# A graph layer's layer norm: centring moved from VectorE to ScalarE, epsilon from GpSimd to VectorE, a negation on GpSimd, and the start-up rearranged

## The reference, cut to what matters

```python
def _layernorm(x, axis=-1, eps=1e-05):
    m = jnp.mean(x, axis=axis, keepdims=True)
    v = jnp.var(x, axis=axis, keepdims=True)
    return (x - m) / jnp.sqrt(v + eps)

def reference(x, adj, W, b):          # x 4096 x 256, adj 4096 x 4096, W 256 x 256
    h = jnp.maximum(_layernorm(x), 0.0)
    out = jax.nn.relu(jnp.matmul(jnp.matmul(adj, h), W.T) + b)
    return x + out
```

## Time and profile before

| what | before |
|---|---|
| median of 3 runs | 383.32 us (382.74 to 383.51) |
| the profiled execution, device time | 382.79 us |
| its span in the trace | 381.0 us |
| PE (TensorE matmuls) busy | 376.3 us, 99% |
| DVE (VectorE) busy | 218.1 us, 57% |
| ACT (ScalarE) busy | 170.9 us, 45% |
| POOL (GpSimd) busy | 63.0 us, 17% |
| granted TensorE clock | 1.00 throughout |

### The profile page before, as it was taken

One profiled execution on the slowest core, in us unless ns is written; L12 is line 12 of the kernel. 1 busy time (PEld: TensorE's weight loads), 2 busy tenths in 40 slices (PEclk: granted clock), 3 DMA queues, 4 the chain that ended last, 5 costly groups with the idle time before them and its releaser, 6 DMA issues.

```text
span 381.0 us, 4425 instructions
## 1 busy us (share of the span) xinstructions
PE 376.3 (99%) x1649; PEld 308.2 (81%) x1649; DVE 218.1 (57%) x293; ACT 170.9 (45%) x197; POOL 63.0 (17%) x79
## 2 busy tenths in 40 slices
PE   8999999999999999999999999999999999999996
PEld 4888888888888888888888888888888888888885
DVE  5999999994745353535564535353565344444424
ACT  4656655654553434343644343434364334343414
POOL 2787777760010000000001000000000100000000
PEclk9999999999999999999999999999999999999999
DMA  7987778669649565656565856565657675656203
GB/s 235 372 288 263 261 267 268 209 201 321 204 156 348 175 214 175 209 179 209 175 207 184 312 178 210 177 211 173 212 174 209 239 255 181 210 181 205 68 2 110
DMA packets 23062, 80.25 MB, mean 211 GB/s; under 512 B 2496, under 2 KB 3264, under 8 KB 23040
## 3 DMA queue, kind: packets, MB, share of 16 engines
q1 hardware_dynamic: 21024, 72.36, 58.0%
q0 software_dynamic: 2016, 7.60, 5.5%
HBM read 75.76 MB, written 4.19 MB: 210 GB/s over the span
## 4 chain that ended last, share of the span: by engine, by line
PE 99%; DVE 0%; ACT 0%; issue 0%
PE bank L379 92%; PE bank L420 6%; PE bank L429 1%; ACT out_sb L355 0%; DVE out_sb L292 0%; DVE warm L256 0%
## 5 line engine op out<-in xcount | busy, mean ns | idle before, releaser
L379 PE MATMUL bank<-adj_hi,h_sb 128*128 128x512 f32 x1024 | 255.1, 390 | 0.0
L223 DVE TENSOR_TENSOR adj_lo<-adj_in,adj_hi 128x1024 fp32r<-128x1024 f32 x126 | 154.2, 1224 | 138.6 <-ACT adj_hi L313 138.5
L379 PEld LDWEIGHTS bank<-adj_hi,h_sb 128*128 128x128 f32 x1024 | 192.3, 188 | 40.7 <-ACT h_sb L323 0.9
L313 ACT ACTIVATE adj_hi<-adj_in 128x1024 fp32r<-128x1024 f32 x126 | 133.4, 1059 | 160.7 <-PE bank L379 157.4
L379 PE MATMUL bank<-adj_lo,h_sb 128*128 128x512 f32 x512 | 137.9, 389 | 0.0
L379 PEld LDWEIGHTS bank<-adj_lo,h_sb 128*128 128x128 f32 x512 | 96.0, 188 | 20.5 <-DVE adj_lo L228 0.6
L203 POOL TENSOR_TENSOR rstd<-var_eps,minus_half 128x1 f32<-128x1 f32 x32 | 49.5, 1546 | 2.5
L215 POOL DMA_DIRECT2D out_t_dram<-out_sb x3 | 2.2, 723 | 209.7 <-DVE out_sb L292 209.7
L323 ACT ACTIVATE h_sb<-centred,rstd 128x256 fp32r<-128x256 f32 x32 | 16.3, 509 | 24.2 <-POOL rstd L203 24.0
L292 DVE TENSOR_TENSOR out_sb<-out_sb,xt_sb 128x512 f32<-128x512 f32 (+1 forms) x17 | 11.1, 659 | 7.7 <-ACT out_sb L355 7.7
L355 ACT ACTIVATE out_sb<-bank,b_sb 128x512 f32<-128x512 f32 (+1 forms) x17 | 11.3, 664 | 9.2 <-PE bank L420 9.2
(11 more groups left out here) (20 smaller groups left out, 31.6 us busy)
## 6 DMA issues: line engine op xcount, KB each, us to landing
adj_in<-adj_t_dram SPq DMA_DIRECT2D x126, 512.0 KB, 3.8
xt_sb<-x_t_dram POOLq DMA_DIRECT2D x4, 1024.0 KB, 7.2
x_sb<-x_dram SPq DMA_DIRECT2D x7, 512.0 KB, 6.5
out_t_dram<-out_sb POOLq DMA_DIRECT2D x3, 1024.0 KB, 5.0
adj_in<-adj_t_dram SPq DMA_DIRECT2D x4, 256.0 KB, 4.3
out_t_dram<-out_sb SPq DMA_DIRECT2D x3, 256.0 KB, 2.0
x_sb<-x_dram SPq DMA_DIRECT2D x4, 128.0 KB, 4.4
w_sb<-w_t_dram POOLq DMA_DIRECT2D x1, 256.0 KB, 5.2
```

The costliest lines, as they stand in the source:

```text
L223: nc.vector.tensor_tensor(adj_lo[:, k, :], adj_in[:, k, :], adj_hi[:, k, :].bitcast(fp32), ALU.subtract).then_inc(s_lo, 1)
L313: nc.scalar.activation(adj_hi[:, k, :], adj_in[:, k, :], ACT.Copy).then_inc(s_hi, 1)
L379: last = nc.tensor.matmul(bank(g, kb, c)[:], h_sb[:, t, hp, kb * P:(kb + 1) * P], adj_parts[ap][:, n % U, chunk(c)], start=(t == 0 and (hp ...
```

## The change

- `centre(t)` goes from VectorE to ScalarE for every tile but the first: Relu(x + minus_mean). The first tile's stays on VectorE.
- GpSimd makes `minus_mean` by a multiplication with -1 of the mean (`negate`), ahead of each root, and no longer adds epsilon. VectorE adds epsilon, on 128x1, behind `bn_aggr`.
- ScalarE's order in the loop becomes `centre(t)`, `h_rounded(t)`, `adj_rounded(t)`.
- In tiles 0 and 1 `h_rounded(0)` goes ahead of the first rounding of adj, and VectorE's `h_rest(1)` ahead of the lo part of tile 1's first chunk.
- The first four transfers are each cut in two by partitions; SyncE issues partitions 0 to 63, ScalarE's queue 64 to 127.
- The small tiles are allocated behind the large ones.

```diff
+        def load_first(engine, rows):
+            for t in range(2):
+                engine.dma_start(x_sb[rows, t, :], x_v[rows, t, :]).then_inc(s_x[t], 16)
+                engine.dma_start(adj_in[rows, 0, chunk(t)], adj_v[rows, 0, chunk(t)]).then_inc(s_early[0][t], 16)
...
-            load_x(0)
-            load_chunk(0, 0)
-            load_x(1)
-            load_chunk(0, 1)
+            load_first(sp, slice(0, HALF))
             load_chunk(1, 0)
             load_chunk(1, 1)
...
+            def negate(t):
+                k = t % U
+                pool.wait_ge(s_mean, t + 1)
+                if t >= U:
+                    pool.wait_ge(s_centred, t - U + 1)
+                nc.gpsimd.tensor_scalar(minus_mean[:, k:k + 1], mean_var[:, k, 0:1], -1.0, None,
+                                        ALU.mult).then_inc(s_minus, 1)

             def root(t):
                 k = t % U
-                pool.wait_ge(s_mean, t + 1)
-                nc.gpsimd.tensor_tensor(var_eps[:, k:k + 1], mean_var[:, k, 1:2], eps_sb[:],
-                                        ALU.add).then_inc(s_var, 1)
                 pool.wait_ge(s_var, t + 1)
...
             for t in range(TILES):
+                if t > 0:
+                    negate(t)
                 root(t)
...
             def moments(t):
                 k = t % U
-                dve.wait_ge(s_x[x_piece(t)], 16)
+                dve.wait_ge(s_x[x_piece(t)], x_steps(t))
                 nc.vector.bn_stats(stats[:, k, :], x_sb[:, t, :]).then_inc(s_stats, 1)
                 dve.wait_ge(s_stats, t + 1)
+                if t > U:
+                    dve.wait_ge(s_minus, t - U)
+                nc.vector.bn_aggr(mean_var[:, k, :], stats[:, k, :]).then_inc(s_mean, 1)
+                dve.wait_ge(s_mean, t + 1)
                 if t >= U:
-                    dve.wait_ge(s_var, t - U + 1)
-                nc.vector.bn_aggr(mean_var[:, k, :], stats[:, k, :]).then_inc(s_mean, 1)
+                    dve.wait_ge(s_rstd, t - U + 1)
+                nc.vector.tensor_scalar(var_eps[:, k:k + 1], mean_var[:, k, 1:2], EPS, None,
+                                        ALU.add).then_inc(s_var, 1)
...
-            for t in range(AHEAD):
-                moments(t)
-                centre(t)
+            moments(0)
+            centre_first()
+            moments(1)
             early_rest(0, 0)
             h_rest(0)
             early_rest(0, 1)
+            h_rest(1)
             early_rest(1, 0)
-            h_rest(1)
             moments(2)
-            centre(2)
             early_rest(1, 1)
             moments(3)
-            centre(3)
             for t in range(EARLY, TILES):
                 adj_rest(t)
                 h_rest(t)
                 if t + AHEAD < TILES:
                     moments(t + AHEAD)
-                    centre(t + AHEAD)
...
+            def centre(t):
+                k = t % U
+                act.wait_ge(s_minus, t)
+                act.wait_ge(s_centred, 1)
+                if t >= U:
+                    act.wait_ge(s_hlo, t - U + 1)
+                nc.scalar.activation(centred[:, k, :], x_sb[:, t, :], ACT.Relu,
+                                     bias=minus_mean[:, k:k + 1]).then_inc(s_centred, 1)
...
+            load_first(act, slice(HALF, P))
+            h_rounded(0)
             early_rounded(0, 0)
-            h_rounded(0)
             early_rounded(0, 1)
+            centre(1)
+            h_rounded(1)
             early_rounded(1, 0)
-            h_rounded(1)
             early_rounded(1, 1)
             for t in range(EARLY, TILES):
+                centre(t)
+                h_rounded(t)
                 adj_rounded(t)
-                h_rounded(t)
```

More of the change, by code:

```diff
@@ L38, in bass_preln_gnn_residual @@
     EARLY = 2
+    HALF = P // 2
     SPLIT_AT = 4
@@ L62, in bass_preln_gnn_residual @@
         w_lo = sb("w_lo", [P, KB, D], fp32r)
[L63 to L69, removed]
         warm = sb("warm", [P, BANK], mybir.dt.bfloat16)
@@ L79, in bass_preln_gnn_residual @@
         out_sb = sb("out_sb", [P, KB, GW])
+        b_sb = sb("b_sb", [P, KB])
+        stats = sb("stats", [P, U, 6])
+        mean_var = sb("mean_var", [P, U, 2])
+        minus_mean = sb("minus_mean", [P, U])
+        rstd = sb("rstd", [P, U])
+        minus_half = sb("minus_half", [P, 1])
+        var_eps = sb("var_eps", [P, U])
         banks = [ctx.enter_context(nc.psum_tensor(f"bank{i}", [P, BANK], fp32)) for i in range(2 * SUMS)]
@@ L88, in bass_preln_gnn_residual @@
         s_xt = sem("xt_landed")
-        s_const = sem("constants_ready")
         s_warm = sem("warm_ready")
@@ L94, in bass_preln_gnn_residual @@
         s_mean = sem("mean_var_made")
+        s_minus = sem("minus_mean_made")
         s_var = sem("var_eps_made")
+        s_const = sem("constant_ready")
         s_rstd = sem("rstd_made")
@@ L145, in product, with x_steps @@
             return bank(g if a == 0 else g + 1, o, c)[:, a:b]
+        def load_first(engine, rows):
+            for t in range(2):
+                engine.dma_start(x_sb[rows, t, :], x_v[rows, t, :]).then_inc(s_x[t], 16)
+                engine.dma_start(adj_in[rows, 0, chunk(t)], adj_v[rows, 0, chunk(t)]).then_inc(s_early[0][t], 16)
+        def x_steps(t):
+            return 32 if t < 2 else 16
         @block.sync
@@ L190, in _ @@
             nc.gpsimd.memset(minus_half[:], -0.5).then_inc(s_const, 1)
-            nc.gpsimd.memset(eps_sb[:], EPS).then_inc(s_const, 1)
-            pool.wait_ge(s_const, 2)
+            pool.wait_ge(s_const, 1)
+            def negate(t):
[5 more added lines that the diff above has]
+                                        ALU.mult).then_inc(s_minus, 1)
             def root(t):
                 k = t % U
-                pool.wait_ge(s_mean, t + 1)
-                nc.gpsimd.tensor_tensor(var_eps[:, k:k + 1], mean_var[:, k, 1:2], eps_sb[:],
-                                        ALU.add).then_inc(s_var, 1)
                 pool.wait_ge(s_var, t + 1)
@@ L232, in moments, with centre_first @@
                 k = t % U
-                dve.wait_ge(s_x[x_piece(t)], 16)
+                dve.wait_ge(s_x[x_piece(t)], x_steps(t))
                 nc.vector.bn_stats(stats[:, k, :], x_sb[:, t, :]).then_inc(s_stats, 1)
                 dve.wait_ge(s_stats, t + 1)
+                if t > U:
+                    dve.wait_ge(s_minus, t - U)
+                nc.vector.bn_aggr(mean_var[:, k, :], stats[:, k, :]).then_inc(s_mean, 1)
+                dve.wait_ge(s_mean, t + 1)
                 if t >= U:
-                    dve.wait_ge(s_var, t - U + 1)
-                nc.vector.bn_aggr(mean_var[:, k, :], stats[:, k, :]).then_inc(s_mean, 1)
[L241 to L246, removed]
+                    dve.wait_ge(s_rstd, t - U + 1)
+                nc.vector.tensor_scalar(var_eps[:, k:k + 1], mean_var[:, k, 1:2], EPS, None,
+                                        ALU.add).then_inc(s_var, 1)
+            def centre_first():
+                nc.vector.tensor_scalar(centred[:, 0, :], x_sb[:, 0, :], mean_var[:, 0, 0:1],
+                                        mean_var[:, 0, 0:1], ALU.max, ALU.subtract).then_inc(s_centred, 1)
             def h_rest(t):
@@ L315, in early_rounded @@
             def early_rounded(t, c):
-                act.wait_ge(s_early[t][c], 16)
+                act.wait_ge(s_early[t][c], 32 if t == 0 else 16)
                 nc.scalar.activation(adj_hi[:, t, chunk(c)], adj_in[:, t, chunk(c)], ACT.Copy).then_inc(s_hi, 1)
+            def centre(t):
[6 more added lines that the diff above has]
+                                     bias=minus_mean[:, k:k + 1]).then_inc(s_centred, 1)
             def h_rounded(t):
```

## The result

The changed kernel takes 390.49 us (median of 5 runs, 389.99 to 390.84) against 383.32 us: a ratio of 1.0195, 95% interval 1.0183 to 1.0206. It is 1.95% slower, and 0.3 us from the forecast of 390.2.

A forecast was written before the change was run, and what follows sets the result against it. TensorE, busy 99% of the span, was taken as the bound, leaving at most about 0.9 us to gain. Start-up 1.11 plus held pairs 5.74 make 6.85 us, on 383.32 giving 390.2 us; range 383.5 to 391.5.

The forecast's parts named there:

- Part 1: VectorE's loop: epsilon (0.07 us) replaces centre (0.33), so the loop shortens from 2.53 to 2.27 us a tile.
- Part 2: Group 0's loop: ScalarE's new order makes adj wait for its own tile's power; 14 held tiles cost 0.41 each, 5.74 us.
- the pair: Two successive tiles in group 0: their splits of adj take 5.85 us together, where TensorE needs 5.44.
- the circle: Group 0: split of k-1 holds GpSimd's negate and power; h_rounded(k), then adj's rounding, wait; split k comes at 3.58 us.
- negate slips in: Rival: negate reads ahead of VectorE's split, pair 5.43 us, no loss per pair; 383.8 us, or 385.7; chance 0.17.
- GpSimd wins: Rival: negate starts first and the split waits 0.17 us for it; pair 5.60, total 386.2 us; chance 0.10.
- Part 3: Start-up: with landings as before, TensorE gets tile 2's lo part at 14.24 instead of 13.13, +1.11 us.
- Part 4: The rest, near nothing: halved first transfers, ScalarE's table load hidden, order of allocation counted at nothing.
- Earlier landing could shift Part 3: Start-up: earlier landing of the halved transfers could shift the start-up term by at most some 0.4 us.
- Part 4, the table load: ScalarE's start: issues end about 2.6, the 1.28 us load at 3.9, ahead of 4.66, so hidden.
- Part 4, the allocation: Small tiles behind the large ones: no row shows an effect of an address, so counted at nothing, gain bounded by 0.9.
- The bound of 0.9 us on a gain: Group 0: no rearrangement of the feeding engines gains over about 0.9 us, as dummy matmuls run until about 6.06.

The follow-up runs named there:

- run 1: Changed kernel with the rounding of adj put back ahead of centre and h_rounded in ScalarE's loop: 383.42 us.
- run 2: Changed kernel with the negation moved from GpSimd to VectorE, behind epsilon: 385.12 us.
- run 3: Kernel before with only h_rounded put ahead of adj_rounded in ScalarE's loop: 387.13 us.
- run 10: Changed kernel with one useless tensor_scalar on 384 elements (the filler) behind each tile's moments in VectorE's loop: 384.92 us.
- run 12: Changed kernel with the moments run three tiles ahead instead of two: 384.85 us.
- run 5: Changed kernel with the first four transfers whole and all on SyncE's queue: 388.92 us.
- run 7: Changed kernel with adj first in ScalarE's loop, first transfers whole on SyncE's queue, and a one-element activation at ScalarE's start for an early table load: 382.23 us.
- run 4: Kernel before with the small tiles allocated behind the large ones: 382.04 us.
- run 9: Kernel before with the small tiles allocated ahead of all large ones, x and W included: 382.07 us.

## Why the prediction was right, and where it wasn't

- **Part 1 was right.** Epsilon put the split 0.07 behind its own start (22.43 to 22.50). VectorE's turn with no wait was 2.28 (20.22 to 22.50), 2.27 in the prediction.
- **Part 2 was right in its mechanism and its size.** The negation was held to 0.08 behind the split's end (0.05 predicted), the power ended 2.05 behind the split's start (2.04), the held split came at 3.57 (3.58), the pair at 5.85 (5.85), TensorE waited 0.44 (0.41). 5.84 us were lost behind tile 2 where 5.74 were forecast. Runs 1, 2, 3, 10 and 12 each open the circle at another place or build it alone, and each came out within 0.6 us of its number.
- **The rival "negate slips in"** had its own pair, 5.43, and didn't happen: the negation started 0.01 ahead of the split and its read came behind it. "GpSimd wins" didn't either: the split wasn't delayed, at a start 0.00 to 0.02 behind the negation's. By recorded starts the rule of the Trainium skill that the prediction quoted (SBUF — State Buffer, "Who interferes with whom") doesn't hold at these distances. Where GpSimd's power started 0.17 to 0.22 ahead (runs 1 and 10) the split didn't hold it, but the split wasn't blocked either, as it would be by the rule: in run 10 it started 0.38 behind the filler and took 1.22, and at 46.38, with no power ahead of it, it did the same, 0.39 and 1.22.
- **Part 3 was mis-sized.** The step that failed is the landings taken as before, together with the hidden table load of Part 4. The lo pass of tile 2 was 2.53 late, not 1.11. Of this, run 5 gives 1.63 to the two queues. What is left, 0.90 (14.03 against 13.13), is near the 1.11, and run 5 goes by the forecast path. "Earlier landing could shift Part 3" had the sign wrong: the bytes came later.
- **Part 4, the table load.** It stood behind the issues, as forecast, but also behind the wait for the first centred tile, from 4.54 to 5.82, not hidden at 2.6 to 3.9. By run 7 that costs nothing measurable without the circle, since h of tile 2 is late anyway. With the circle it wasn't tried; in run 5, where the load runs from 4.00 to 5.28, it lies on the chain.
- **Part 4, the allocation.** Counted at nothing; it gains 0.56 by the chain and 0.6 by run 4. The bound of 0.9 held it.
- **The bound of 0.9 us on a gain was worked out too low.** The dummy matmuls don't last until 6.06: run 7's first real one starts at 5.70, behind 0.63 of idle TensorE. The 0.6 of the allocation isn't feeding at all and comes on top. No run had both, and none gained more than 0.9.
- **So the close forecast is in part a cancellation:** the start was 1.4 too small, the products with W 0.6 too large, the pairs 0.1 too small. By the traces the sum should have been 7.8 where it said 6.85, and the step from the profiled executions to the medians hid 0.6 of the rest. That the forecast came within 0.3 us is luck; the circle's own term, 5.74 against 5.84, is not.

The best of these kernels are those with the small tiles moved and nothing else (runs 4 and 9, 382.04 and 382.07) and run 7 (382.23). All beat both kernels, by 0.1 to 0.2% of the kernel before.

## What to carry to other kernels

Before an instruction that waits is put ahead of one that doesn't, count the circle it closes: from the moment its input is made, through every engine, to the next time that engine can start. Here one line moved on ScalarE, which before the change was idle for 43% of group 0 (53.60 of the 94 us from 16 to 110 busy), cost 7 us of 383 (run 1), because the circle became one tile long and went through GpSimd. An engine freed of work may also start its next instruction sooner and hold a neighbour that used to slip through; a lighter VectorE made GpSimd's part of the circle longer, and run 10 undid that with useless work.

## What the runs showed of the hardware

- A GpSimd instruction on 128x1 that starts 0.00 to 0.02 us ahead of a VectorE instruction with two SBUF inputs, by the recorded starts, is held for the whole of it: the negation took 1.31 instead of 0.22, the power 1.64 instead of 0.56. A power 0.17 ahead took 0.57 (run 1). The boundary lies between; the durations put it at 0.14, where the read would be, which is worked out and not seen.
- A VectorE `tensor_scalar` that reads one tile held GpSimd too: the power of run 10 ended 0.42 behind the filler's end. In the kernel before, an addition that started 0.05 behind `centre` took 0.19 as when free. What decides here wasn't tried.
- Between the split and `h_rest`, which follow each other without a gap, GpSimd got in with one instruction only: held by the split, the negation ended 0.08 behind it, and the power that followed was held again by `h_rest`, to 0.43 behind its end.
- With half-partition transfers from two issuing queues each issue was longer, 0.57 to 0.88 us against 0.42, and they landed later than whole ones from one queue: the second chunk of adj at 7.95 or 7.00 against about 6.1.
- The same matmuls took 233 or 227 ns by where small tiles lay between the weights' and the moving operand's tiles; moving them out to either side gave 0.6 us.
